# Four image layers in one kernel: the joint between the scan and the box layer with a five-slot group buffer, loads inside the scan, and skip rows added by TensorE

## The reference

```python
# L2: tokens are 2x2 windows, D = 48*4 = 192 features, L = 64*64 = 4096 tokens
h = dA * h + (d_l * u_l)[:, :, None] * B_l[:, None, :]        # scan over the tokens
y = jnp.einsum('bdn,bn->bd', h, C_l)
...
y = ys.transpose(1, 2, 0)                                     # [192, 4096]
y = y + D_param[None, :, None] * u.transpose(0, 2, 1)         # the skip rows
y = y * (z * jax.nn.sigmoid(z))                               # z is 1: a constant factor
out = y.reshape(Bb, NS, NS, PC, w, w).transpose(0, 3, 1, 4, 2, 5)
...
x = x + L2(_gn(x))
x = x + L3(_gn(x))   # L3: two 3x3 convolutions give boxes and scales; box means are read from an integral image
```

## Time and profile before

| | |
|---|---|
| median of 3 runs | 7394.66 us (7393.37 to 7396.27) |
| profiled execution, its own time | 7441.44 us |
| its span, first to last instruction | 7432.1 us |
| mean granted TensorE clock | 0.942 of full speed |
| busy over the span | PE 82%, DVE 90%, ACT 70%, POOL 46% |
| scan and its y extraction end, last store issued | about 6555 us of the span |
| joint block | about 6557 to 6623 us |
| group norm and box layer | 6623 to 7432 us |

### The profile page before, as it was taken

How to read it: one execution, slowest core, us unless ns; L and a number is a source line. 1 busy time by engine, 2 the same in 40 slices (tenths; PEclk the granted TensorE clock), 3 DMA queues, 4 the chain that set the end, 5 groups by cost and what they waited for, 6 DMA issues and landing times. The chain is left out here.

```text
span 7432.1 us, 168927 instructions
## 1 busy us (share of the span) xinstructions
PE 6066.0 (82%) x69188; PEld 2637.1 (35%) x69188; DVE 6674.6 (90%) x5678; ACT 5237.4 (70%) x5319; POOL 3451.3 (46%) x1801
## 2 busy tenths in 40 slices
PE   6899999999999999898778888888888888867000
PEld 3433333333333333465223333333333333335000
DVE  8899999999999999799689999999999999966654
ACT  3488888888888888433578888888888888832000
POOL 2000000000000000000389999999999999935777
PEclk9999999999999999999899999999999999978555
DMA  3200000000000000000200000000000000032322
GB/s 67 57 13 9 10 9 9 11 11 10 9 9 9 12 9 7 6 7 8 69 12 6 6 6 6 6 6 6 6 6 6 6 6 6 6 80 65 83 75 74
DMA packets 145341, 153.63 MB, mean 21 GB/s; under 512 B 66140, under 2 KB 125308, under 8 KB 143132
## 3 DMA queue, kind: packets, MB, share of 16 engines
q1 hardware_dynamic: 118624, 89.43, 4.8%
q0 software_dynamic: 24576, 50.36, 2.6%
q10 hardware_dynamic: 1440, 3.75, 0.3%
HBM read 101.83 MB, written 37.95 MB: 19 GB/s over the span
## 5 line engine op out<-in xcount | busy, mean ns | idle before, releaser
L1891 POOL TENSOR_TENSOR k_image<-k_image,s_b 128x1024 f32<-128x1024 f32 x1152 | 2702.7, 2357 | 116.3 <-ACT k_image L1804 82.9
L797 ACT ACTIVATE att_prob<-att_scores,a_bound,a_temp 128x1024 f32<-128x1024 f32 x2048 | 2356.7, 1202 | 361.7 <-PE att_scores L747 361.7
L808 DVE TENSOR_TENSOR att_prob_lo<-att_prob 128x1024 f16<-128x1024 f32 x2048 | 2440.0, 1237 | 169.2 <-ACT att_prob L797 158.9
L732 POOL TENSOR_TENSOR k_image<-k_image,att_rden 48x512 f32 x32 | 68.6, 2143 | 2894.4 <-DVE att_rden L829 2894.4
L1804 ACT COPY k_image<-h_du 128x1024 f32<-128x1024 f32 x1152 | 1166.4, 1013 | 322.6 <-PE h_du L1738 322.3
L1854 DVE TENSOR_TENSOR_SCAN h_state_odd<-h_keep,k_image 128x1024 f32<-128x1024 f32 x576 | 1321.7, 2331 | 0.3 <-ACT h_keep L1810 0.3
L1810 ACT ACTIVATE h_keep<-h_keep,h_decay 128x1024 f32<-128x1024 f32 x1152 | 1256.7, 1091 | 74.8 <-PE h_keep L1727 51.2
L747 PE MATMUL att_scores<-att_queries,att_keys 32*128 32x512 f16 (+1 forms) x20480 | 1292.9, 377 | 19.1 <-DMA att_keys<-qk_halves 16.5
L764 PE MATMUL att_sums<-att_prob,a_values 128*64 128x512 bf16 x8192 | 1129.4, 396 | 0.0
L1727 PE MATMUL h_keep<-h_rows,h_spread 128*128 128x512 bf16 x2304 | 698.2, 385 | 513.4 <-DVE h_state_odd L1854 263.2
L1738 PE MATMUL h_du<-h_rows,h_spread 128*128 128x512 bf16 x2304 | 699.7, 385 | 35.3 <-DMA h_rows<-parts 33.3
(11 more groups left out here) (311 smaller groups left out, 6377.5 us busy)
## 6 DMA issues: line engine op xcount, KB each, us to landing
y_rows<-h_y_sb SPq DMA_DIRECT2D x1024, 3.0 KB
att_queries<-qk_halves SPq DMA_DIRECT2D x124, 128.0 KB, 2.2
parts<-t_part SPq DMA_DIRECT2D x48, 192.0 KB, 2.5
h_rows<-parts SPq DMA_DIRECT2D x128, 72.0 KB
b_shared<-cells,b_index POOLq DMA_INDIRECT x512
qk_halves<-qkv_hi SPq DMA_DIRECT2D x128, 48.0 KB, 1.6
cells<-b_shared SPq DMA_DIRECT2D x4, 1536.0 KB, 5.1
att_keys<-qk_halves SPq DMA_DIRECT2D x32, 128.0 KB, 2.7
```

The source lines that it names most:

```text
L797: nc.scalar.activation(prob[:, u % RING, :], scores[:, u % SLOTS_S, :], ACT.Exp, bias=bound[:, 0:1], scale=temp[:, 0:1]).then_inc(prob_rea ...
L808: nc.vector.tensor_tensor(prob_lo[:, u % RING, :], prob[:, u % RING, :], prob_hi[:, u % RING, :], ALU.subtract).then_inc(low_ready, 1)
L1891: nc.gpsimd.tensor_tensor(drive[k % 3], du_sb[k % 3], b[:, c * CH:(c + 1) * CH], ALU.mult).then_inc(drive_ready, 1)
```

## The change

- `b0` and `b1` of the scan now lie in one tile `lent` (128 x 8192) that outlives the layer. After the last drive multiplication of POOL it serves as a buffer with `JOIN_SLOTS` = 5 slots, each for a group of y and a group of skip rows; the box layer later puts its table chunks, its gathered rows and `act1` there.
- SP issues the loads of groups 0 to 4 inside the scan block, between the stores of the last chunk but one and the stores of the last chunk. Only groups 5 to 7 are loaded in the joint.
- ACT gives back three quarters of the image instead of two when the recurrence is done, and the fourth at the end of the scan block.
- The ten loads of tables and weights move from SP's queue to ACT's, at the start of the joint.
- POOL's eight additions go. PE turns y and skip rows with two plain f32 matmuls for each place, the second accumulating on the first, where there was one transpose. `y_summed` goes.
- DVE's addition walks the pixels in another order (the two columns of the windows outside, the windows inside).

```diff
+def join_buffers(lent, g):
+    two = lent[:, g % JOIN_SLOTS * 2 * PER * D:(g % JOIN_SLOTS + 1) * 2 * PER * D].rearrange("p (s k f) -> p s k f", s=2, f=D)
+    return two[:, 0], two[:, 1]
+
+def load_group(eng, lent, y_rows, skip_rows, y_loaded, g):
+    k = slice(g * PER, (g + 1) * PER)
+    for dst, rows in zip(join_buffers(lent, g), (y_rows, skip_rows)):
+        src = rows.rearrange("d l -> (d l)").rearrange("(k p f) -> p k f", p=P, f=D)
+        eng.dma_start(dst, src[:, k, :]).then_inc(y_loaded[g % JOIN_SLOTS], 16)
...
-            for c in range(NCH - 2, NCH):
-                for half in range(2):
-                    store(NG - 1, c, half)
+            for half in range(2):
+                store(NG - 1, NCH - 2, half)
+            sp.wait_ge(drive_ready, NG * STEPS)
+            for half in range(2):
+                sp.wait_ge(y_stored[half], (NG - PER) * NCH * 64)
+            for g in range(JOIN_SLOTS):
+                load_group(sp, lent, y_rows, skip_rows, y_loaded, g)
+            for half in range(2):
+                store(NG - 1, NCH - 1, half)
             for stored in y_stored:
                 sp.wait_ge(stored, NG * NCH * 64)
...
-            for k in range(2):
+            def give_back(k):
                 px = slice(k * NPIX // 4, (k + 1) * NPIX // 4)
                 act.dma_start(image[HI, W + px.start:W + px.stop], kept_image[:, px]).then_inc(returned[k], 16)
+            for k in range(3):
+                give_back(k)
             for half in range(2):
                 copy_y(NG - 1, NCH - 1, half)
+            act.wait_ge(drive_ready, NG * STEPS)
+            act.wait_ge(selected, NG * NCH * UNITS_Y // 2)
+            give_back(3)
...
-                for g in range(2, NSUM):
-                    sp.wait_ge(y_turned, (g - 1) * PER)
-                    load(g)
+                for g in range(JOIN_SLOTS, NSUM):
+                    sp.wait_ge(y_turned, (g - JOIN_SLOTS + 1) * PER)
+                    load_group(sp, lent, y_rows, skip_rows, y_loaded, g)
...
                     if k % PER == 0:
-                        pe.wait_ge(y_summed, g + 1)
+                        pe.wait_ge(y_loaded[g % JOIN_SLOTS], 32 * (g // JOIN_SLOTS + 1))
                     if k >= 4:
                         pe.wait_ge(y_added, 2 * (k - 3))
                     for place in range(4):
-                        src = y_in[:, g % 2, k % PER, :].rearrange("p (c q) -> p q c", q=4)[:, place]
-                        last = nc.tensor.transpose(turned_y[:, k % 4, place, :], src, ident[:, :])
+                        for part, rows in enumerate(join_buffers(lent, g)):
+                            src = rows[:, k % PER, :].rearrange("p (c q) -> p q c", q=4)[:, place]
+                            last = nc.tensor.matmul(turned_y[:, k % 4, place, :], src, ident[:, :], start=part == 0,
+                                                    stop=part == 1)
...
-                            "c (y a x b) -> c a y x b", a=WIN, b=WIN, x=NT)[:, a]
-                        src = turned_y[:, k % 4, 2 * a:2 * a + 2, :].rearrange("c b (y x) -> c y x b", x=NT)
+                            "c (y a x b) -> c a y b x", a=WIN, b=WIN, x=NT)[:, a]
+                        src = turned_y[:, k % 4, 2 * a:2 * a + 2, :].rearrange("c b (y x) -> c y b x", x=NT)
```

More of the change, by code:

```diff
@@ L1335, in scan_layer @@
         ln = Names(nc, layer, "s")
-        b_c = [ln.sb(name, [P, L]) for name in ("b0", "b1", "c0", "c_even", "c_odd")]
+        b_c = [lent[:, 0:L], lent[:, L:2 * L]] + [ln.sb(name, [P, L]) for name in ("c0", "c_even", "c_odd")]
         project_tokens(nc, image, gmean, norm, sems, d, b_c, parts, skip_rows, kept, stats)
         returned = [ln.sem(f"returned{k}") for k in range(4)]
-        scan(nc, image, d, b_c, parts, y_rows, kept_image, returned)
-    return y_rows, skip_rows, kept_image, returned
+        y_loaded = [ln.sem(f"y_loaded{k}") for k in range(JOIN_SLOTS)]
+        scan(nc, image, d, b_c, parts, y_rows, skip_rows, kept_image, returned, lent, y_loaded)
+    return y_rows, skip_rows, returned, y_loaded
 def project_tokens(nc, image, gmean, norm, sems, d, b_c, parts, skip_rows, kept, stats):
@@ L1615, in _, with scan @@
             finish(nblk - 1)
-def scan(nc, image, d, b_c, parts, y_rows, kept_image, returned):
+def scan(nc, image, d, b_c, parts, y_rows, skip_rows, kept_image, returned, lent, y_loaded):
     with ExitStack() as ctx:
@@ L1916, with box_layer @@
 OUT_BANKS = 2
-NTILE, PER = L // P, 4
-NSUM = NTILE // PER
-def box_layer(nc, image, gmean, norm, sems, ident, d, stats, out, y_rows, skip_rows, kept_image, returned):
+def box_layer(nc, image, gmean, norm, sems, ident, d, stats, out, lent, y_rows, skip_rows, returned, y_loaded):
     cells = nc.dram_tensor("cells", [NPIX, PAIR_ROW], F32, kind="Internal").ap()
@@ L1973, in box_layer @@
             ps_s = jn.ps("ps_s", [SPAN, BLK])
-            y_v, skip_v = (t.rearrange("d l -> (d l)").rearrange("(k p f) -> p k f", p=P, f=D) for t in (y_rows, skip_rows))
-            sum_rows = lambda t, g: t[:, g % 2, :, :].rearrange("p k f -> p (k f)")
             @block.scalar
             def _(act):
-                for k in range(2, 4):
-                    px = slice(k * NPIX // 4, (k + 1) * NPIX // 4)
-                    act.dma_start(image[HI, W + px.start:W + px.stop], kept_image[:, px]).then_inc(returned[k], 16)
+                act.wait_ge(cleared, 3)
+                for dst, src in ((w1[:, :, LO], d["w1_off"]), (w1[:, :, HI], d["w1_mod"]), (b1[LO, :], d["b1_off"]),
+                                 (b1[HI, :], d["b1_mod"]), (w2[LO, 0:4], d["w2_off"]), (w2[HI, 4:HEADS], d["w2_mod"]),
+                                 (b2[:, 0:4], d["b2_off"].partition_broadcast(P)),
+                                 (b2[:, 4:HEADS], d["b2_mod"].partition_broadcast(P)),
+                                 (tri[:, :, :], d["triangle"]), (centre[:, :, :], d["centre"])):
+                    act.dma_start(dst, src).then_inc(loaded, 16)
                 act.wait_ge(loaded, 160)
@@ L2024, in _ @@
                     clear(t[:, :, :])
-                add_skip(2)
-                pool.wait_ge(loaded, 160)
-                add_skip(3)
+                for px in pads:
+                    clear(x_split[:, px])
                 pool.wait_ge(absolute, 1)
@@ L2636, in program @@
         patch_filter_layer(nc, image, gmean, norm, sems, ident, d, stats, kept_image, kept)
-        rows = scan_layer(nc, image, gmean, norm, sems, ident, d, stats, kept_image, kept)
-        box_layer(nc, image, gmean, norm, sems, ident, d, stats, out, *rows)
+        lent = n.sb("lent", [P, 2 * L])
+        rows = scan_layer(nc, image, gmean, norm, sems, ident, d, stats, kept_image, kept, lent)
+        box_layer(nc, image, gmean, norm, sems, ident, d, stats, out, lent, *rows)
 def kernel(**inputs):
```

47 lines of the change are left out of this document (9 added, 38 removed).

## The result

| | before | after |
|---|---|---|
| median us (20 runs each, same chip) | 7395.07 (7391.61 to 7397.42) | 7408.68 (7405.53 to 7413.38) |
| ratio to before | | 1.0019 [1.0013, 1.0026] |
| last recurrence to last statistics of the joint | 83.4 and 83.9 (two profiles) | 103.0 |

The account below looks back on a forecast made before the run. The joint was taken as bound first by a DMA wait, then by DVE at 1.25 us a tile, after the change by PE. 4.1 + 14.0 = 18.1 us on 7394.66 gave 7413, eight-in-ten range 7402 to 7421.

Parts of the forecast that it names:

- The joint opens late: End of scan block: last y stores wait behind ten loads, so the joint opens at 6579 and PE starts +4.1 us later.
- the two bounds: End of the last group load before the joint: 6574.5 from adding rates, 6578.2 from the mixed rate; 6577 taken.
- The pace: Joint: sixteen PE records a tile, 512 spaced 0.112 us, make PE the bound; 61.9 us instead of 47.9, +14.0.
- Costs at nothing: Joint: ACT's weight loads, POOL's clears, the image's third and fourth quarters and DVE's pixel order add zero.
- The sum: Whole kernel: 4.1 + 14.0 = 18.1 us slower, with gn3 and the box layer as long as now.
- fair sharing: Rival, loads before the joint: groups and image share engines evenly, PE starts at 6569.2; +8, 7403; chance 0.10.
- Stores not held: Rival, end of scan block: loads do not delay the stores, block ends at 6557 as now; +2.4, 7397; chance 0.03.
- Matmuls that do not show: Rival, joint: paired matmuls overlap, a tile costs PE under 1.25 us, DVE sets pace; +1.5 to +3, 7397; chance 0.03.
- The longer case: Rival, joint: clock stays low, matmuls exceed two records, or loads end after 6583; above 7420; chance 0.09.
- the likeliest case: Joint: opening 6576.5 to 6580.7, spacing 0.110 to 0.116, low clock 3.4 to 5 us; +14 to +22; chance 0.72.
- fourfold advantage for transposes in f32: Joint, PE: by the skill's rule a tile would cost 3.6 us, near +74 us in all; the prediction said the trace disagrees.
- the two terms: Joint: late opening from loads ahead of the stores, +4.1 us, and PE's pace from two-record f32 matmuls, +14.0 us.

Follow-up runs that it names:

- e5: Changed kernel with only two groups loaded ahead of the last stores of y, groups 2 to 4 in the joint: +5.8 us against before, 1.0009.
- e6: Changed kernel with all stores of y ahead of the loads, two groups behind them in the scan block: +4.3 us against before, 1.0005.
- e3: Kernel before with only PE adding the skip rows by plain f32 matmuls, no sums on POOL: +10.0 us against before, 1.0012.
- e4: Changed kernel with each piece of y transposed twice instead of the matmuls, skip rows left out of the result: -1.5 us against before, 0.9999.
- e10: e9 with DVE's old order of pixels: 7429.85 us, -13.2 us against before, 0.9983.
- e2: Changed kernel with the sums back on POOL and four transposes a tile, loads as in the change: +3.7 us against before, 1.0004.
- e8: Changed kernel with image and groups on SP's queue in order of use, sums on POOL, transposes on PE: -7.4 us against before, 0.9990.
- e1: Kernel before, unchanged, profiled a second time: 7395.77 us in one execution.
- e11: e8 without POOL's sums, skip rows added by PE with plain f32 matmuls: -12.2 us against before, 0.9984.
- e7: e6 with the sums on POOL and four transposes a tile: -6.2 us against before, 0.9992.
- e9: e8 with POOL's first five sums ahead of the weights and the last clear behind all sums: 7429.63 us, -13.4 us against before, 0.9981.

## Why the prediction was right

The forecast was 7413 with a likeliest range of 7408 to 7417; 7408.68 lies in it, near its lower edge. By the joint alone it would have been 7414; a difference outside the joint, which nobody forecast, takes off 5.5 us (below). The prediction gave 0.72 to a slowdown beyond 15 us, its limit of what can be told from no change; 13.6 is under that, yet with 20 executions of each kernel the interval [1.0013, 1.0026] tells it apart. Step by step:

- **The joint opens late** (forecast +4.1, measured from the last recurrence +5.8: 41.3 against 35.5). The stores were issued at 6569.60, behind ten loads, and the block opened near 6576.8. The last group landed before 6575 (the DMA share falls from 1.08 to 0.46 in the microsecond from 6574 and is 0.00 in the next), 2 to 3 us ahead of the forecast 6577, so the estimate between the two bounds was good. But the stores' issue ended only at 6572.54 and SP waited 3.7 us more for them to land instead of the 1.5 of the earlier trace rows, and the kernel reached its last recurrence 4.1 us earlier than the first profile of before (6535.48 against 6539.59), so the same absolute time is a later start. e5 and e6 show the mechanism.
- **The pace** (forecast 61.9 us, +14.0; measured 61.7, +13.9 against the earlier trace rows). Two records for each f32 matmul, 512 in all, spaced 0.109 to 0.110. The low clock lasted until 6582.7 or so (the clock of that microsecond is 0.64), near 6 us from PE's start instead of 4; the smaller spacing pays for it. e3 shows this term alone (+12.5), e4 that it goes when matmuls become transposes.
- **Costs at nothing**: the pixel order (e10), confirmed. Weight loads on ACT, POOL's clears and the image's quarters, confirmed for the change, since PE waits for none of them and DVE only for PE; not a property of them: in e2 and e8, where sums stand behind the weights, POOL waits 4.9 and 17.9 us for these.
- **The sum** was 18.1 us; the joint measures 19.1 longer than in e1, and the time 13.6. What is between lies outside the joint. Against e1 the changed trace reaches the last recurrence 1.1 us earlier and takes 768.4 instead of 773.4 us behind the joint: -1.1 + 19.1 - 5.0 = +13.0, the difference of the two spans (7406.9 and 7393.9). The prediction took what lies ahead as left alone and what lies behind "as long as now", and this is the step whose size was off.

Two traces of it lie in code that the change does not touch. Ahead of the joint it is the projection (line 1470, 1452 in before). Its 128 matmuls into `t_ps_b` take 131.0 us from the first to the last in the changed trace, where the slowest has 612 ns, and 134.1 in e1 and e3, where the slowest have 1059 and 1056.

```profile
L1470 PE MATMUL t_ps_b<-k_image,t_w_bc x128: 609/611/612, 3552.4 to 3683.4; 112*128 x96, 112*128 112x512 f32 x32
```

It is not tied to the changed code: e6, built on the change, has 1058 ns and 134.2 us as well. Behind the joint, 3.3 of the 5.0 us have arisen 67 us on, at the last matmul into `b_ps_w` (63.4 us behind the last statistics, 66.7 in e1). In the ten microseconds that start 30 us behind the statistics PE's granted clock is 0.66 in e1 and 1.00 in the changed trace:

```profile
6650.50:6660.50 10.00, 9.55 (x37) 5.57 (x38) 5.57 (x6) 1.06 (x3) 0.00 (x0) 0.66 0.33 138
6668.50:6678.50 10.00, 9.72 (x48) 5.17 (x47) 5.52 (x6) 4.08 (x6) 0.00 (x0) 1.00 0.37 157
```

This is not tied to the change either: e6 and e11 take 66.8 and 66.7 us to that matmul. What the single traces differ by outside the joint thus goes partly with where the clock is low. But in the medians too the time of every kernel built on the changed one is 1.9 to 5.9 us less than its joint says, that of e3, built on before, 0.7. Why stays open.

The 46.8 us between profile and median that the prediction carried over fit the difference of two chips: e1 was profiled at 7395.77 us.

The rivals: fair sharing (a start at 6569) is out, the stores were still queued then. Stores not held is out (e5, e6). Matmuls that do not show are out (e3). The longer case is out; 6 us of low clock were just beyond the likeliest case's 3.4 to 5. The Trainium skill's fourfold advantage for transposes in f32 ("TensorE: Matmul & The Clock Gate", section "Terms") would be seen in e4 against the change: the trace shows one record against two of equal length, a factor of two.

Together e2 to e4 part the two terms: taking away only the matmuls leaves the late start (+5.9 and a sum), taking away only the early loads leaves the pace. The starts add up (+7.7 in e2 and -1.8 in e3 give the change's +5.9), the ends not quite: +5.6 and +10.7 make 16.3, where the change has 19.1. With the sums on POOL the five slots shorten what follows PE's start by 2.2 us (46.4 against 48.5), and under the matmuls' pace this shows nowhere.

## What to carry to other kernels

A load issued early is not early for what stands behind it in its queue, nor for the end of its block, even from behind the stores (e6): ask what the queue still has to issue when the last store is ready. In e8 to e11 four group loads and one quarter of the image stand ahead of the last stores without holding them: the loads were issued before these stores were ready, and in e8 the block ends at 18.0 us, in before at 17.5. Put large transfers in one queue in the order of their use: here PE starts 12 to 13 us earlier for it with either way of adding the skip rows. With matmuls the end followed (91.1 to 77.6 us); with sums only when POOL's order changed too (80.7 in e7 and e8, 74.0 in e9). Moving an addition to TensorE for nothing holds only if its records fit under the engine that sets the pace; count f32 matmuls as two records, transposes as one. When a wait disappears, look at which order on the next engine was harmless only because of it, as POOL's sums behind the weights were.

## What the runs showed of the hardware

- The issue of the fourth group load in a row held SP's queue for 10.68 us (16.51 in e5, 8.08 in e6), while three quarters of the image were in flight; in e9, with one quarter, the four of groups 0 and 1 took 0.4 to 1.3 us. Not only stores behind loads but the issues themselves are held.
- The image's rows (16 KB on 48 partitions) beside group pieces of 768 B give 128 to 170 GB/s at a DMA share of 0.91 to 1.08; the groups alone 326. The image without the groups has 158, so the low rate is the image's own and not one of mixing; no run shows which of its properties makes it.
- Ten small tables and weights, issued while loads of groups and image were in flight, landed 8.0 to 18.8 us after their issue in e8 and e9; in the change, with the engines nearly empty, 1.6 to 3.3.
- A plain f32 matmul of 48 weight columns and 128 moving leaves two records, a transpose of the same shape one, each of 272 ns at granted clock 1.00; back to back the matmuls' records are spaced 0.110 us at that clock.
- The granted clock rose to 1.00 some 6 us after PE's start from idle in the change, 4 us in before.
